# Computing the normalization's shift on GpSimd instead of VectorE, with new orders of work, in a graph attention layer

## The reference

```python
def _layernorm(x, axis=-1, eps=1e-05):
    m = jnp.mean(x, axis=axis, keepdims=True)
    v = jnp.var(x, axis=axis, keepdims=True)
    return (x - m) / jnp.sqrt(v + eps)
...
    q = _heads(seq_inputs @ Wq + bq)
    k = _heads(seq_inputs @ Wk + bk)
    v = _heads(seq_inputs @ Wv + bv)
    scores = jnp.einsum('bhqd,bhkd->bhqk', q, k) / np.sqrt(HEAD_SIZE)
    bias = jnp.where(graph_mask, 0.0, NEG)[:, None]
    probs = jax.nn.softmax(scores + bias, axis=-1)
    ctx = jnp.einsum('bhqk,bhkd->bhqd', probs, v)
    return ctx @ Wf + bf
h = jnp.maximum(_layernorm(x, axis=-1), 0.0)
x = x + _L0_gnn_ref(h, ..., adj)
```

## Time and profile before

| | us |
|---|---|
| median of 3 runs | 470.89 |
| lowest and highest | 469.98, 471.25 |
| the profiled execution | 470.06 |
| its span, first to last instruction | 468.1 |

### The profile page before, as it was taken

The page is one execution under the profiler, slowest core; times in us unless marked ns, Lnnn a source line. Parts: engine busy times, 40 slices in busy tenths (PEclk is TensorE's granted clock), DMA queues, the critical chain, the costliest instruction groups (busy, mean ns, idle before and its releaser), DMA issues.

```text
span 468.1 us, 12797 instructions
## 1 busy us (share of the span) xinstructions
PE 455.7 (97%) x4449; PEld 272.0 (58%) x4450; DVE 372.0 (79%) x740; ACT 364.4 (78%) x822; POOL 305.9 (65%) x308
## 2 busy tenths in 40 slices
PE   6989999999999999999999999999999999999996
PEld 2754656565565655656565565656556565555664
DVE  5999988878886886968688696886969687786964
ACT  5779899976979698795968969587796685996760
POOL 4279487875767857576684857747674866464682
PEclk9999999999999999999999999999999999999999
DMA  8256669999995979969597695967999875796996
GB/s 295 71 100 132 128 131 173 215 198 184 204 198 118 194 174 148 213 145 221 117 210 168 146 221 122 216 157 136 188 157 195 154 156 129 138 147 156 173 176 211
DMA packets 219614, 78.55 MB, mean 168 GB/s; under 512 B 199472, under 2 KB 219568, under 8 KB 219568
## 3 DMA queue, kind: packets, MB, share of 16 engines
q1 hardware_dynamic: 209200, 65.63, 72.1%
q10 hardware_dynamic: 10368, 12.33, 9.5%
HBM read 16.19 MB, written 12.58 MB: 61 GB/s over the span
## 4 chain that ended last, share of the span: by engine, by line
PE 84%; ACT 4%; DMA 3%; DVE 3%; issue 2%; SPq 2%; POOL 1%; ACTq 0%; DVEq 0%; POOLq 0%
PE ps L1068 26%; PE ps L1069 26%; PE ps L1070 26%; PE ps L1130 6%; ACT masked L791 1%; DMA w_raw<-in_Wk 1%; SPq L613 1%; DMA ht_parts<-h_pairs 1%; DVE masked L918 1%; DMA ct_parts<-ctx_parts 1%; ACT qkt_hi L777 1%; ACT h_sb L768 1%; ACT h_pairs L766 1%; POOL h_pairs L678 0%; POOL probs_parts L693 0%
## 5 line engine op out<-in xcount | busy, mean ns | idle before, releaser
L693 POOL TENSOR_TENSOR probs_parts<-masked,probs_parts 128x768 f16<-128x768 f32 x64 | 105.0, 1648 | 54.5 <-ACT probs_parts L806 54.3
L791 ACT ACTIVATE masked<-masked,neg_max 128x128 f32<-128x128 f32 x384 | 118.7, 391 | 19.7 <-DVE neg_max L927 18.5
L1068 PE MATMUL ps<-ht_parts,w_hi 128*128 128x512 f16 (+1 forms) x315 | 111.8, 361 | 1.4 <-DMA ht_parts<-h_pairs 1.0
L1070 PE MATMUL ps<-ht_parts,w_lo 128*128 128x512 f16 (+1 forms) x315 | 111.9, 361 | 0.0
L1069 PE MATMUL ps<-ht_parts,w_hi 128*128 128x512 f16 (+1 forms) x315 | 111.9, 361 | 0.0
L899 DVE SCALAR_TENSOR_TENSOR qkt_lo<-ps,bias_qk,qkt_hi 128x512 f16<-128x512 f32 x96 | 68.6, 742 | 13.9 <-ACT qkt_hi L777 13.8
L699 POOL TENSOR_TENSOR ctx_parts<-ctx_sb,ctx_parts 128x384 f16<-128x384 f32 x62 | 56.8, 921 | 33.5 <-ACT ctx_parts L812 33.0
L688 POOL TENSOR_TENSOR x_bf<-x_sb,b_out 128x384 f32<-128x384 f32 x64 | 63.2, 999 | 23.0 <-DVE y_sb L950 22.9
L777 ACT ACTIVATE qkt_hi<-ps,bias_qk 128x512 f16<-128x512 f32 x96 | 62.8, 677 | 13.1 <-PE ps L1070 13.0
L918 DVE SCALAR_TENSOR_TENSOR masked<-ps,score_unscale,mask 128x384 f32<-128x384 f32 x128 | 70.9, 609 | 1.3 <-PE ps L1130 1.3
L678 POOL TENSOR_TENSOR h_pairs<-h_sb,h_pairs 128x384 f16<-128x384 f32 x60 | 56.5, 949 | 15.1 <-ACT h_sb L768 14.8
(11 more groups left out here) (92 smaller groups left out, 902.5 us busy)
## 6 DMA issues: line engine op xcount, KB each, us to landing
x_sb<-in_x ACTq DMA_DIRECT2D x56, 192.0 KB, 2.8
y<-y_sb SPq DMA_DIRECT2D x56, 192.0 KB, 2.6
x_sb<-in_x SPq DMA_DIRECT2D x8, 192.0 KB, 5.7
y<-x_bf SPq DMA_DIRECT2D x8, 192.0 KB, 3.3
pt_parts<-probs_parts SPq DMA_TRANSPOSE x64, 4.1
ct_parts<-ctx_parts SPq DMA_TRANSPOSE x62, 3.0
adj_sb<-in_adj ACTq DMA_DIRECT2D x14, 64.0 KB, 2.4
w_raw<-in_Wk SPq DMA_DIRECT2D x1, 576.0 KB, 6.4
```

What stands on the lines that cost most here:

```text
L693: nc.gpsimd.tensor_tensor(probs_parts[b][:, 1, :], probs[b], probs_parts[b][:, 0, :], ALU.subtract).then_inc(probs_split, 1)
L791: last = nc.scalar.activation(masked[b][:, u, :], masked[b][:, u, :], ACT.Exp, bias=neg_max[b][:, u:u + 1])
L1068: nc.tensor.matmul(to, a_hi, b_hi, start=first, stop=False)
L1070: return nc.tensor.matmul(to, a_lo, b_hi, start=False, stop=last)
```

## The change

The shift leaves DVE. POOL's `inverse` now makes it in two products: the mean times a constant tile of minus ones into `neg_mean`, as soon as the moments are there, and after the power `neg_mean` times `rstd` into `shift_by`. It waits for its own earlier results in between. DVE's stage `shift` disappears from all tables. Almost every turn in the tables has a new number; the numbers of banks stay.

What the new numbers mean for the order within each queue:

- Groups 4 to 9 (the loop): PE, ACT, POOL and SP have the same order as before, and DVE's is the same without `shift`.
- PE at the start: the second `turn_first` stands directly behind the first, both short `keep_busy` behind it, and the second `sum_rows` behind the third turn. `project_v` 0.2 has no `keep_busy` before it. `weigh_values` 0.0 moves in front of `project_v` 1.1, and 0.2 in front of `project_qk` 2.3.
- DVE at the start: `additive_mask` 0, `qk_lo` 0.0 and `reduce_rows` 2 stand in front of the last three `weight_rest` of Wv, and `qk_lo` 0.1 in front of the last `scale`.
- ACT at the start: `exponentials` 0.2 and 0.3 stand together in front of `probs_hi` 0.2 and 0.3; `weight_hi` 10 and 11 stand behind `exponentials` 1.0. POOL: the last `weight_lo` stands behind `normed_lo` 3.1.
- DVE at the end: largest_score 13.0 and 13.1, mask_scores 13.2, normalize_ctx 12.2, values_lo 13.1, mask_scores 13.3, statistics 15.0, additive_mask 14 and 15, statistics 15.1 and 15.2, largest_score 13.2 and 13.3, statistics 15.3, aggregate 15, qk_lo 14.0 and 14.1.
- ACT at the end: qk_hi 14.0 and 14.1, probs_hi 13.0 and 13.1, exponentials 13.2, values_hi 13.2, qk_hi 14.2, values_hi 13.3, ctx_hi 12.2, qk_hi 14.3, normalize 15.0, probs_hi 13.2, ctx_hi 12.3, normalize 15.1 to 15.3, qk_hi 14.4 and 14.5.
- POOL at the end: probs_lo 13.0, `inverse` 15, probs_lo 13.1, ctx_lo 12.2 and 12.3, residual 14.0, normed_lo 15.0 to 15.3, probs_lo 13.2 and 13.3.
- PE at the end: project_qk 14.0 to 14.3, project_v 13.2 and 13.3, project_qk 14.4, weigh_values 12.3, project_out 12.0 and 12.1, weigh_values 13.0, project_qk 14.5, project_v 14.0, weigh_values 13.1, scores 14; later weigh_values 13.2 and 13.3 stand directly behind project_qk 15.0, and project_out 13.0 in front of project_qk 15.4.

The diff, with the tables cut to the common one and parts of those for groups 0, 14 and 15:

```diff
@@ -40,10 +40,10 @@
 TURNS = {
     "scores": (0, 10, 20), "project_v": (30, 60, 70, 100), "project_out": (10110, 10140, 10190, 20040),
     "project_qk": (-9950, -9920, -9870, -9850, -9830, -9820), "weigh_values": (160, 200, 10090, 10120),
-    "normalize_ctx": (240, 10000, 10140, 10180), "mask_scores": (10, 20, 70, 80), "largest_score": (30, 60, 90, 130),
-    "values_lo": (40, 110, 120, 170), "finish": (10200, 10210, 10320, 20050),
-    "statistics": (-29700, -29690, -19900, -19850), "aggregate": (-19840,), "shift": (-19810,),
-    "qk_lo": (-9780, -9770, -9740, -9730, -9720, -9710), "additive_mask": (-19750,),
+    "normalize_ctx": (230, 10000, 10140, 10180), "mask_scores": (10, 20, 70, 80), "largest_score": (30, 60, 90, 130),
+    "values_lo": (40, 110, 120, 170), "finish": (10190, 10200, 10310, 20050),
+    "statistics": (-29710, -29700, -19900, -19850), "aggregate": (-19840,),
+    "qk_lo": (-9790, -9780, -9750, -9740, -9730, -9720), "additive_mask": (-19760,),
     "ctx_hi": (290, 10000, 10140, 10210), "values_hi": (10, 50, 80, 120), "exponentials": (20, 40, 100, 150),
     "load": (-29810, -29780, -19970, -19940), "probs_hi": (70, 90, 170, 300),
     "qk_hi": (-9890, -9870, -9770, -9760, -9740, -9730), "normalize": (-19840, -19820, -19800, -19750),
...
     0: {
-        "keep_busy": (39040, 39070, 39230), "sum_rows": (39050, 39090, 39150, 39200),
-        "turn_first": (39060, 39080, 39100, 39110), "first_q": (39120, 39130, 39140, 39160),
-        "scale": (38300, 38460, 38490, 38640), "first_lo": (38320, 38410, 38420, 38430),
-        "weight_rest": (38360, 38380, 38390, 38500, 38510, 38520, 38570, 38600, 38610, 38360, 38360, 38360),
-        "scale_bias": (38400, 38550), "reduce_rows": (38450, 38450, 38580),
-        "qk_lo": (38620, 38650, 38660, 38680, 38700, 38710), "additive_mask": (38630,),
+        "keep_busy": (39040, 39080, 39090), "sum_rows": (39050, 39110, 39160, 39210),
+        "turn_first": (39060, 39070, 39100, 39120), "first_q": (39130, 39140, 39150, 39170),
+        "scale": (38350, 38490, 38540, 38690), "first_lo": (38400, 38460, 38470, 38510),
+        "weight_rest": (38430, 38440, 38450, 38550, 38560, 38570, 38650, 38660, 38670, 38430, 38430, 38430),
+        "reduce_rows": (38500, 38500, 38640), "additive_mask": (38610,),
+        "qk_lo": (38630, 38680, 38700, 38710, 38730, 38750), "values_lo": (38720, 38740, 38800, 38830),
...
     14: {
-        "project_qk": (-39300, -39270, -39260, -39250, -39200, -39190),
-        "statistics": (-39230, -39220, -39200, -39190), "aggregate": (-39170,), "shift": (-39140,),
-        "largest_score": (-38690, -38660, -38620, -38610), "normalize_ctx": (-38510, -38500, -38390, -38330),
-        "finish": (-38320, -38290, -38260, -38210), "qk_hi": (-39010, -38950, -38940, -38890, -38880, -38860),
-        "normalize": (-39210, -39160, -39140, -39130), "values_hi": (-38850, -38770, -38700, -38560),
-        "ctx_hi": (-38600, -38570, -38530, -38480), "inverse_deviation": (-39590,),
+        "project_qk": (-39300, -39290, -39280, -39270, -39240, -39190),
+        "statistics": (-39270, -39230, -39220, -39210), "aggregate": (-39190,), "additive_mask": (-38950,),
+        "normalize_ctx": (-38540, -38520, -38430, -38350), "finish": (-38330, -38320, -38310, -38250),
+        "qk_hi": (-39010, -39000, -38950, -38920, -38850, -38840), "normalize": (-39190, -39180, -39170, -39120),
+        "inverse_deviation": (-39600,), "normed_lo": (-39580, -39570, -39530, -39520),
...
     15: {
-        "project_qk": (-49100, -49090, -49080, -49060, -49050, -48990),
-        "turn_ctx": (-48760, -48750), "statistics": (-49050, -48940, -48930, -48920), "aggregate": (-48910,),
-        "shift": (-48840,), "qk_lo": (-48580, -48570, -48560, -48550, -48490, -48470), "additive_mask": (-48530,),
-        "turned_ctx_hi": (-48410, -48400), "inverse_deviation": (-49460,),
+        "project_qk": (-49090, -49060, -49050, -49040, -49020, -48990),
+        "turn_ctx": (-48760, -48750), "statistics": (-48960, -48930, -48920, -48890), "aggregate": (-48880,),
+        "turned_ctx_hi": (-48410, -48400), "inverse_deviation": (-49450,),
...
@@ -263,7 +262,7 @@
 LAST_TURN = STEP * (LOOP + 2 * REPS)
 
 
-PROLOGUE = {"load": 2, "load_mask": 2, "aggregate": 1, "inverse_deviation": 1, "shift": 1,
+PROLOGUE = {"load": 2, "load_mask": 2, "aggregate": 1, "inverse_deviation": 1,
             "normalize": 1, "transpose_normed": 2, "normed_lo": 1}
 
 ONCE = ("keep_busy", "turn_first", "first_q", "sum_rows", "project_bias", "transpose_second", "output_bias",
@@ -445,6 +444,8 @@
         bf_rows = sb("bf_rows", [P, H])
         b_out = sb("b_out", [P, H])
         minus_half = sb("minus_half", [P, B])
+        minus_one = sb("minus_one", [P, B])
+        neg_mean = sb("neg_mean", [P, B])
         eps = sb("eps", [P, B])
         table_loader = sb("table_loader", [P, B])
 
@@ -545,6 +546,7 @@
         var_eps_ready = sem("var_eps_ready")
         rstd_ready = sem("rstd_ready")
         shift_ready = sem("shift_ready")
+        mean_negated = sem("mean_negated")
         h_ready = sem("h_ready")
         first_h_ready = sem("first_h_ready")
         h_split = sem("h_split")
@@ -665,12 +667,21 @@
                     .then_inc(rstd_ready, 1)
 
             def inverse(group, item, i):
+                par = group % 2
                 pool.wait_ge(moments_ready, parted(group, i))
+                if group == 1:
+                    pool.wait_ge(consts_set, 7)
+                nc.gpsimd.tensor_tensor(neg_mean[:], moments[par][:, :, 0], minus_one[:], ALU.mult)\
+                    .then_inc(mean_negated, 1)
                 inverse_deviation(group, slice(0, B), i)
                 pool.wait_ge(var_eps_ready, parted(group, i))
                 if group >= 2:
                     wait_normed(pool, group - 2, B - 1, i)
                 inverse_root(group, slice(0, B), i)
+                pool.wait_ge(mean_negated, nth(1, group - 1, 0, i))
+                pool.wait_ge(rstd_ready, parted(group, i))
+                nc.gpsimd.tensor_tensor(shift_by[par][:], neg_mean[:], rstd[par][:], ALU.mult)\
+                    .then_inc(shift_ready, 1)
 
             def normed_lo(group, b, i):
                 pool.wait_ge(h_ready, nth(B, group - 1, b, i))
@@ -730,6 +741,7 @@
             pool.wait_ge(consts_set, 5)
             nc.gpsimd.affine_select(out=identity[:], in_=plain_ones[:], pattern=[[-1, P]], compare_op=ALU.is_equal,
                                     fill=0.0, base=0, channel_multiplier=1).then_inc(identity_set, 1)
+            nc.gpsimd.memset(minus_one[:], -1.0).then_inc(consts_set, 1)
             run_turns(pool, {
                 "inverse_deviation": inverse, "normed_lo": normed_lo, "residual": residual, "probs_lo": probs_lo,
                 "ctx_lo": ctx_lo, "first_inverse": first_inverse, "set_ones": set_ones, "bias_sum": bias_sum,
@@ -875,17 +887,6 @@
                 for b in range(B):
                     last = nc.vector.bn_aggr(moments[group % 2][:, b, :], stats[:, b, :])
                 last.then_inc(moments_ready, 1)
-
-            def shift_graphs(par, at):
-                nc.vector.scalar_tensor_tensor(out=shift_by[par][:, at], in0=moments[par][:, at, 0], scalar=-1.0,
-                                               in1=rstd[par][:, at], op0=ALU.mult, op1=ALU.mult)\
-                    .then_inc(shift_ready, 1)
-
-            def shift(group, item, i):
-                dve.wait_ge(rstd_ready, parted(group, i))
-                if group >= 3:
-                    dve.wait_ge(h_ready, nth(B, group - 3, B - 1, i))
-                shift_graphs(group % 2, slice(0, B))
 
             def additive_mask(group, item, i):
                 dve.wait_ge(adj_loaded[group % 2], by_parity(group, i))
@@ -1032,7 +1033,7 @@
                                                op1=ALU.subtract).then_inc(first_h_split, 1)
 
             run_turns(dve, {
-                "statistics": statistics, "aggregate": aggregate, "shift": shift, "additive_mask": additive_mask,
+                "statistics": statistics, "aggregate": aggregate, "additive_mask": additive_mask,
                 "qk_lo": qk_lo, "values_lo": values_lo, "mask_scores": mask_scores, "largest_score": largest_score,
                 "normalize_ctx": normalize_ctx, "finish": finish,
                 "turned_ctx_lo": turned_ctx_lo, "output_bias": output_bias, "reduce_rows": reduce_rows, "column_bound": column_bound,
```

297 lines of the change are left out of this document (149 added, 148 removed).

## The result

The changed kernel takes 466.56 us by the median of six executions (465.29 to 468.03) beside 470.57 us for the kernel before: a ratio of 0.9914, with a 95% interval of 0.9889 to 0.9938. It is 4.0 us faster. 469.9 us had been forecast, in a range that ended at 468.2. The profiled execution is the longest of the six, 468.03 us with a span of 466.3.

What follows compares the result with a forecast made beforehand. It took PE to bound the kernel, full from 57 to 385 us. Start -0.2, end -1.0 and new waits +0.2 summed to -1.0 us, taking the median 470.89 to 469.9 us, range 468.2 to 471.9.

Steps and rivals of the forecast that it cites:

- The middle is full, so DVE's time there is worth 0: Between 57 and 385 us PE is busy throughout, so work taken from DVE there buys nothing.
- POOL's two products cost nothing: Per group POOL gets some 0.5 us more, which fits in the middle and costs 0.
- Of the other five, two stand ahead of a wait of PE: Ten of 15 shifts lie in the full window, worth 0; of the rest only groups 1's and 15's precede PE waits.
- -0.2 at the 0.8 us wait: Start, PE's wait on the last weight scale: dropped shift 0.94 us, added q/k low half 0.76, net -0.2 us.
- The 1.0 us wait on the transposes stays: Start, group 1's transposed h: PE's 1.0 us wait stays, 1.0 us either way with one transpose's landing.
- Rule and row: Shared GpSimd/VectorE port rule, up to 1.4 us DVE time per meeting shift; worth was read from PE's waits instead.
- The end, -1.0 at the scores of group 14: End: ACT's reordered work fills its idle time, closing PE's 1.0 us wait; -1.0 us, between -1.0 and 0.
- The final 1.2 us wait stays: Very end: PE's wait for a context transpose, 3.95 us behind SP's queue, stays and moves with PE.
- New waits, +0.2: End: group 13's last probabilities, out.13.0 and scores 15 come late for PE; 0.2 us, ends 0 and 1.5.
- Sum: Whole kernel: start, end and new waits total -1.0 us, median 470.89 becoming 469.9 us; chance 0.43.
- The start gives as well: Rival: before 57 us the 0.8 us scale wait goes and the 1.0 us transposes wait halves; 468.8 us, chance 0.25.
- POOL stands still: Slower rival: POOL waits in front of aggregate 15, delaying group 13's second probabilities; 472.6 us, chance 0.13.

Runs made afterwards that it cites:

- vector_rest: Kernel before's orders, VectorE computing the shifts of the twelve groups other than 1, 2 and 15, GpSimd those three; 466.04 us, ratio 0.9931 to before.
- dummy_op: order_before plus, at each old place of the shift, an unread VectorE operation of its form that waits only for the moments; 466.89 us, ratio 0.9930 to before.
- pool_pause: Kernel before, all shifts on VectorE, plus two unread products on GpSimd behind group 1's root; 469.33 us, ratio 0.9976 to before.
- order_before_busy: order_before with nine matmuls of keep_busy at the old place, between the first and second transpose of h; 465.69 us, ratio 0.9902 to before.
- before_again: The kernel before once more, unchanged, for a second profile; 469.45 us, ratio 0.9985 to before.
- order_before: Changed kernel with the shift on GpSimd but the old orders before and behind the loop; 466.49 us, ratio 0.9925 to before.
- vector_15: order_before with VectorE computing the shift of group 15 alone, at its old place; 467.00 us, ratio 0.9938 to before.
- start_new: Shift on GpSimd, the changed kernel's new order up to the loop, old order behind it; 465.66 us, ratio 0.9904 to before.
- mended: Changed kernel with nine keep_busy matmuls, not one, between h's first two transposes, and additive mask 4 behind group 2's last v_lo; 466.81 us, ratio 0.9940 to before.
- busy_only: Changed kernel with nine keep_busy matmuls, not one, between the first and second transpose of h, mask unmoved; 465.89 us, ratio 0.9907 to before.

## Why the prediction was wrong, step by step

- **The middle is full, so DVE's time there is worth 0.** Right. vector_rest puts twelve shifts back for 0.1 to 0.3 us, and dummy_op puts fifteen operations of up to 1.6 us on VectorE for none.
- **POOL's two products cost nothing.** Right: 195 to 286 ns each for 0.19 to 0.48 bounded, and no wait of PE hangs on them in the middle (ACT waits 1.6 us in 2 times for the shift there, behind which PE stays fed).
- **"Of the other five, two stand ahead of a wait of PE."** This step failed, and it is the largest miss in kind. Only three of the 15 shifts lie outside the full window, those of groups 1, 2 and 15; groups 3 and 4, at 60.8 and 93.6 us, are inside it like the ten. The one that I left out, at a price of 0, is group 2's. The list of waits names only what comes last. Group 2's shift stood behind two waits that hid it, and once these go it costs 1.2 us of waiting by itself. I should have looked at each of these shifts with what ran beside it: the longest, 1.59 us, is group 2's, at 41.09 us.
- **Start: "-0.2 at the 0.8 us wait".** The term was mis-sized: the start gives some 2.3 us at full clock. I priced the shift at its 0.94 us, took off a low half of q/k that the new order puts in its place, and let the operations behind it keep the lengths of the earlier trace rows, as if these were their own. They depend on what GpSimd runs meanwhile: in pool_pause the mask returned 0.38 us as well. With the old order, where nothing takes the shift's place, the scale's wait went too, so the order was not what mattered.
- **"The 1.0 us wait on the transposes stays."** Wrong, though the text gave it 1.0 us either way. It is gone in the profile after and in all others with group 1's shift on GpSimd but one (order_before_busy, 0.8 us, a landing of 4.87). It is also gone in before_again, with the shift on VectorE and a landing of 3.93. So it hangs on this landing as well, which took 2.7 to 5.4 us over all profiles, and what sets that is open.
- **Rule and row.** The Trainium skill's rule on the shared port was given its size (up to 1.4 us a shift) and then no term of the sum, because I read the worth from PE's waits and saw one behind two shifts only. The runs show what was missing between rule and sum: a shift that VectorE takes up at the root's end meets GpSimd's next operation where GpSimd has one ready. That was so at four of the 15, and it cost time at the two of them, groups 1 and 2, that lie before 57 us. The two in the full window cost nothing that vector_rest shows.
- **The end, -1.0 at the scores of group 14.** Right in size (1.2 us measured between the scores of groups 13 and 14) and in its times: forecast and measured, aggregate 397.5 and 396.9, shift 399.4 and 398.8, normalization 400.3 and 400.0, sixth high half done 407.5 and 407.3, low half 408.3 and 408.1, PE 408.8 and 408.5. Wrong in the reason: I ascribed it to ACT's new order filling the 3.70 us of idle time. In order_before, with ACT's old order, the wait is gone as well, since a shift on GpSimd follows the root by 0.2 us instead of standing seven turns down VectorE's queue. vector_15 shows the converse: ACT's 3.7 us and PE's 1.0 us are back by that one shift.
- **"The final 1.2 us wait stays."** Wrong: the wait fell to 0.2 us. I explained the 3.95 us by the queue of transposes in front; in the fourteen profiles in which no instruction packet falls into this transpose it takes 3.0 us. The packet was not in my reckoning, and whether it makes the transpose longer stays open.
- **New waits, +0.2.** The term was too small in the profiled execution: 1.1 us on v at 93 and 102 us. They hold back the gain of the start: PE is 1.6 us ahead at the scores of group 2 (76 us) and 0.2 us at those of group 3 (103 us), at a lower clock in the start. Waits on v in the middle, 0.6 to 1.1 us together, are in four profiles with the new start orders (after, start_new, mended, busy_only); with the old ones there are 0.2 us at most (vector_15), though PE is 3.0 us ahead in dummy_op. So they belong to the new orders, not to an early PE alone.
- **Sum.** -1.0 forecast, -4.0 measured; by experiments at full clock -3.7 to -4.1 for the engine (2.4 to 2.6 at groups 1, 2 and 15, the rest behind the scores of group 15 and not resolved) and nothing that can be told from zero for the orders. "The start gives as well" (468.8) was nearest, with the right place and half of the size (1.3 us of some 2.3); "POOL stands still" did not occur: its wait before group 15's products was 1.41 us.
